# Gating and summing the 16 states of a scan: one wide multiply and one strided reduction in place of 31 narrow operations

## The reference, cut to what matters

```
L, D_MODEL, D_INNER, D_STATE = 2048, 1024, 2048, 16
xz = x @ in_proj_w.T ; x_ssm, z = split(xz)
xc = silu(causal_conv(x_ssm, width 4))
dt_r, Bv, Cv = split(xc @ x_proj_w.T)          # 1, 16 and 16 columns
dt = softplus(dt_r @ dt_proj_w.T + dt_proj_b)
h_t[d, n] = exp(dt_t[d] * A[d, n]) * h_{t-1}[d, n] + dt_t[d] * B_t[n] * xc_t[d]
y_t[d]    = sum over the 16 n of  h_t[d, n] * C_t[n]
y = (y + xc * D) * silu(z) ; out = y @ out_proj_w.T
...
src = layer_norm(src + attention(src))
src = layer_norm(src + relu(src @ W1 + b1) @ W2 + b2)
```

## Time and profile before

| what | us |
|---|---|
| median of 11 runs | 7879.23 (7842.57 to 7989.63) |
| the profiled execution's own time | 7878.18 |
| its span on its slowest core (core 1) | 7876.3 |
| spans of its 8 cores | 7788.7 to 7876.3 |
| VectorE busy | 3911.0 |
| TensorE busy | 2939.3 |
| ScalarE busy | 1959.3 |
| scans L715, first to last start | 368.7 to 3578.6 |

### The profile page before, as it was taken

The page is one execution under the profiler, slowest core; times in us unless marked ns, Lnnn a source line. Parts: engine busy times, 40 slices in busy tenths (PEclk is TensorE's granted clock), DMA queues, the critical chain, the costliest instruction groups (busy, mean ns, idle before and its releaser), DMA issues.

```text
span 7876.3 us, 45497 instructions; the slowest of 8 cores (7788.7 to 7876.3 us)
## 1 busy us (share of the span) xinstructions
PE 2939.3 (37%) x11136; PEld 1122.2 (14%) x11136; DVE 3911.0 (50%) x5725; ACT 1959.3 (25%) x2902; POOL 339.2 (4%) x639
## 2 busy tenths in 40 slices
PE   6300020001100020003506777777757637558272
PEld 3100000000000010001202222222212212223131
DVE  6299947996599839993302221222213343321414
ACT  4223313222233223232213333333330000011112
POOL 0100010001000010000000000000000000000000
PEclk9655565556655575556757777777767768767686
DMA  3400051002300060003781111111111111121211
GB/s 67 52 0 0 0 77 15 0 0 33 59 0 0 3 90 0 0 0 82 83 104 25 20 18 22 17 21 22 21 27 43 55 49 49 42 67 43 75 64 50
DMA packets 100622, 275.49 MB, mean 35 GB/s; under 512 B 19144, under 2 KB 23500, under 8 KB 99084
## 3 DMA queue, kind: packets, MB, share of 16 engines
q0 software_dynamic: 57168, 178.17, 14.6%
q1 hardware_dynamic: 33980, 77.64, 3.2%
q10 hardware_dynamic: 9216, 16.78, 0.6%
HBM read 321.74 MB, written 63.25 MB: 49 GB/s over the span
## 4 chain that ended last, share of the span: by engine, by line
DVE 35%; PE 31%; issue 11%; DMA 10%; ACT 8%; another core or an unknown queue 2%; SPq 1%; DVEq 1%; ACTq 0%; POOL 0%; POOLq 0%
DVE h_band L715 16%; PE psF L1300 6%; PE psF L1519 6%; PE psF L1327 5%; ACT attT L1339 4%; DVE h_band L727 4%; PE psF L1719 3%; PE psF L1731 3%; DMA xreD<-xin 2%; PE psF L1314 2%; DMA wzD<-winp_z 2%; DVE h_band L736 2%; DVE xc_a L1571 2%; PE psF L908 1%
## 5 line engine op out<-in xcount | busy, mean ns | idle before, releaser
L715 DVE TENSOR_TENSOR_SCAN h_band<-daD,hcol,dxD 128x512 f16<-128x512 f32 x1024 | 1302.9, 1278 | 2.3
L626 ACT ACTIVATE daD<-dtD,c_A 128x512 f32<-128x512 f32 x1024 | 732.4, 721 | 1827.7 <-DVE h_band L715 1817.6
L593 PE MATMUL psA<-woD,xc_a 128*128 128x512 bf16 x256 | 69.9, 397 | 2762.4 <-DVE xc_a L765 2726.9
L1339 ACT ACTIVATE attT<-psF 128x1024 bf16<-128x1024 f32 x512 | 498.3, 1022 | 630.8 <-PE psF L1314 624.6
L1388 DVE TENSOR_TENSOR ost<-psF,rlbG 64x512 bf16<-64x512 f32 x64 | 42.4, 680 | 1130.2 <-DMA rlbG<-lrow 547.2
L1300 PE MATMUL psF<-wvG,act_a 128*128 128x512 bf16 x2048 | 491.5, 395 | 175.7 <-DVE ost L1388 147.1
L1519 PE MATMUL psF<-xc_a 128*128 128x512 bf16 x2048 | 475.2, 397 | 30.7 <-DVE xc_a L1571 30.7
L1314 PE MATMUL psF<-qT_aug,kT_aug 65*128 65x512 bf16 x1024 | 381.6, 478 | 208.1 <-ACT attT L1339 204.9
L710 DVE TENSOR_TENSOR dxD<-uD,bb_sb 128x512 bf16<-128x512 bf16 x960 | 407.7, 425 | 95.6 <-DVE h_band L715 2.8
L593 PEld LDWEIGHTS psA<-woD,xc_a 128*128 128x128 bf16 x256 | 22.4, 100 | 2806.8 <-issue 2790.3
L1327 PE MATMUL psF<-attT,v_aug 128*65 128x512 bf16 x1024 | 379.1, 551 | 88.2 <-ACT attT L1339 88.2
(11 more groups left out here) (218 smaller groups left out, 3604.1 us busy)
## 6 DMA issues: line engine op xcount, KB each, us to landing
xc_a<-wob POOLq DMA_DIRECT2D x128, 256.0 KB, 4.7
wzD<-winp_z POOLq DMA_DIRECT2D x64, 256.0 KB, 3.8
woD<-woutT POOLq DMA_DIRECT2D x64, 256.0 KB, 4.7
wob<-wo POOLq DMA_DIRECT2D x1, 16384.0 KB, 298.5
wvG<-wv POOLq DMA_DIRECT2D x32, 512.0 KB, 6.0
xc_a<-w1b POOLq DMA_DIRECT2D x64, 256.0 KB, 6.6
xc_a<-w2b ACTq DMA_DIRECT2D x64, 256.0 KB, 7.9
xreD<-xin SPq DMA_DIRECT2D x16, 512.0 KB, 6.0
```

The lines of the kernel that those rows point to most:

```text
L626: inc(s.activation(daD[n % 2][:], dt[:], AF.Exp, scale=c_A[:, dc * NN + n: dc * NN + n + 1]), "da")
L715: last = v.tensor_tensor_scan(h_band[:, n * TW:(n + 1) * TW], daD[n % 2][:], dxD[n % 2][:], hcol[:, dc * NN + n: dc * NN + n + 1], op0=OP. ...
L1339: inc(s.activation(attT[:, (2 * grp) * 512:(2 * grp + 2) * 512], psF1[:, slot:slot + 1024], AF.Exp, scale=0.125), "gs")
```

## The change

On VectorE, the 16 multiplies become one over the whole 128 x 8192 tile. The 15 additions become one `tensor_reduce` with fp32 output: it reads `h_band` through a pattern whose inner index walks the 16 states of one time step, 512 elements (1024 bytes) apart, and whose outer index walks the 512 time steps. All products are still rounded to fp16; the sum is no longer rounded between additions.

On TensorE, the wait for `ov` 256 ahead of the feed-forward block and the waits for `e3s` inside its loops (4 and 8 in the first half, 12 and 16 in the second) become one wait for `e3s` 16 ahead of it.

```diff
@@ VectorE, for each (tc, dc) @@
-                fg = [0] * NN
-                for n in range(NN):
-                    fg[n] = inc(v.tensor_tensor(h_band[:, n * TW:(n + 1) * TW],
-                                                h_band[:, n * TW:(n + 1) * TW],
-                                                cb_sb[:, n * TW:(n + 1) * TW],
-                                                op=OP.mult), "vf")
-                fl1 = [0] * 8
-                for i8 in range(8):
-                    wge(v, "vf", fg[2 * i8 + 1])
-                    if i8 >= 1:
-                        wge(v, "vf", fl1[i8 // 2])
-                    fl1[i8] = inc(v.tensor_tensor(
-                        h_band[:, i8 * TW:(i8 + 1) * TW],
-                        h_band[:, 2 * i8 * TW:(2 * i8 + 1) * TW],
-                        h_band[:, (2 * i8 + 1) * TW:(2 * i8 + 2) * TW], op=OP.add), "vf")
...
-                wge(v, "vf", fl2[3])
-                f31 = inc(v.tensor_tensor(y_sl[:], h_band[:, 2 * TW:3 * TW],
-                                          h_band[:, 3 * TW:4 * TW], op=OP.add), "vf")
-                wge(v, "vf", f31)
-                fy = inc(v.tensor_tensor(y_sl[:], y_sl[:], h_band[:, 0:TW],
-                                         op=OP.add), "vf")
+                fg = inc(v.tensor_tensor(h_band[:], h_band[:], cb_sb[:],
+                                         op=OP.mult), "vf")
+                wge(v, "vf", fg)
+                fy = inc(v.tensor_reduce(
+                    y_sl[:],
+                    bass.AP(h_band[:].tensor, h_band[:].offset,
+                            [h_band[:].ap[0], [1, TW], [TW, NN]]),
+                    axis=AX.X, op=OP.add), "vf")
                 wge(v, "szs", tc * DC + dc + 1)
                 wge(v, "vf", fy)
@@ TensorE, feed-forward block @@
-        wge(t, "ov", 256)
+        wge(t, "e3s", 16)
         for sh in range(2):
             for r in range(4):
                 ri = sh * 4 + r
                 wge(t, "hw0", 16 * 8 * (ri + 1))
                 wge(t, "hw1", 16 * 8 * (ri + 1))
                 for sc in range(2):
-                    wge(t, "e3s", sh * 8 + (sc + 1) * 4)
                     for m in range(8):
```

More of the change, by code:

```diff
@@ L740, in _ @@
[L740 to L749, removed]
@@ L750, in _ @@
-                f30 = inc(v.tensor_tensor(h_band[:, 0:TW], h_band[:, 0:TW],
-                                          h_band[:, TW:2 * TW], op=OP.add), "vf")
-                wge(v, "vf", fl2[3])
-                f31 = inc(v.tensor_tensor(y_sl[:], h_band[:, 2 * TW:3 * TW],
-                                          h_band[:, 3 * TW:4 * TW], op=OP.add), "vf")
-                wge(v, "vf", f31)
-                fy = inc(v.tensor_tensor(y_sl[:], y_sl[:], h_band[:, 0:TW],
-                                         op=OP.add), "vf")
+                fg = inc(v.tensor_tensor(h_band[:], h_band[:], cb_sb[:],
+                                         op=OP.mult), "vf")
```

## The result

The changed kernel is slower: ratio of the times 1.0537, 95% interval 1.0502 to 1.0571 (medians 8318.58 us of 12 runs against 7901.66 us of 47 runs of the kernel before, both taken over all executions; the ratio leaves out the clearly slower ones, in which TensorE's granted clock was lower, so it isn't the quotient of the medians). The forecast was 8356 us.

The account below looks back on a forecast made before the run. No engine bounds the whole kernel; VectorE paces the scan stage. Per pair 4.56 (multiply) + 15.00 (reduction) - 12.09 (removed) = +7.47 us, times 64 = +478, on 7878 gives 8356 us, range 7945 to 8510.

Parts of the forecast that it names:

- What bounds the scan stage: Scan stage: VectorE sets the pace, ScalarE has slack; L626 waited 1817.6 us on VectorE, L715 idled 2.3 us.
- the stretch: VectorE at each pair's end, first product to L760: 12.09 us, 64 times on the path, to grow to 19.6.
- The multiply: VectorE, one multiply over 8192 columns: 4.46 us, 4.56 with its wait, against 5.38 before; 0.82 us gained.
- The reduction: VectorE, 8192 elements read with 1024-byte jumps at 1.8 ns each: 14.90 us, 15.00 with its wait.
- readings of the carry L721: Carry copy, 16 elements in 176 ns, taken three ways: 2.0, 1.9 or 1.1 ns per element under the jump.
- The free jump: Rival on VectorE's reduction: jumps cost nothing, 8.69 us, +81 us in all, 7959 us; chance 0.28.
- Two elements per step: Rival on VectorE's reduction: two 16-bit elements per step, 4.46 us, -190 us in all, 7688 us; chance 0.03.
- Nothing was hidden: Rival in the scan stage: ScalarE sets the pace, VectorE's longer tail fills waiting time, 7878 us; chance 0.02.
- The jump of more than 2.1 ns: Rival on VectorE's reduction: from 2.1 ns per element it takes 17.35 us, the kernel 8513; chance 0.07.
- The waits: Two per pair on VectorE, both counted; TensorE's feed-forward entrance wait costs nothing, covered by `w2b` loads by 20 us.
- The sum: Scan stage, per pair 4.56 + 15.00 - 12.09 = +7.47 us, times 64 = +478 us, giving 8356 us.

Follow-up runs that it names:

- the run over neighbours: Changed kernel with its reduction reading 16 neighbouring elements per output instead of 16 lying 1024 bytes apart (other sums than the reference's): ratio 1.0094.
- the second timing: Only TensorE's waits at the feed-forward block changed, against the kernel before, timed again after a first 1.0039: ratio 1.0000, interval 0.9976 to 1.0023.

## Why the prediction was right

The time was forecast as 8356 us, and the mechanism was the right one, but the value of its deciding term came near the measured one by luck, as shown under the reduction.

**What bounds the scan stage.** Right. L715's idle time stayed at 2.4 us, L626's wait on VectorE grew from 1817.6 to 2199.0, and the last L593 of core 1 moved from 3632.9 to 4036.8 us, +404 where the stretch says +408. No block hid more than a few us of it.

**The multiply.** Forecast 4.46 us, measured 4.42. It goes at (4425 - 1224) / 6144 = 0.52 ns per column, half the 1.04 of a reduction, and the gain of 0.8 us per pair that was set against the reduction is real: by itself it makes the kernel faster.

**The reduction.** This was the term that decided, and the term that was off: 14.90 us forecast, 13.83 measured, a price of (13834 - 150) / 8192 = 1.67 ns per element where 1.8 was taken. That is 1.07 us per pair, 68 us in all. The mechanism, a price at every jump, held: 0.63 ns on top of 1.04. The way to the number didn't. The 1.8 was chosen from readings of the carry L721 that took 15 to 30 of its 176 ns for reads slowed by the jump, and a copy of 16 neighbours takes 174 to 175 ns as well. Most of what the readings gave to the jump was therefore start. A copy of 16 elements can't tell 1.8 from 1.04, and that the value came within 8% was luck. The prediction also calls the rows that it compared like with like (one source, fp32 out); the longest of them, L1170, writes bf16, and all of them read fp32 where L721 reads fp16. The figure of 1.73 that the prediction quotes from the Trainium skill was the closer one. Row L721 doesn't agree with it in two readings out of three, as was said; it says nothing on it. The chance of 0.60 is given for a price from 1.5 ns, while its own range begins at 1.6; nothing here hangs on that.

**The rivals.** The free jump, with 0.28 the strongest rival, was excluded by the mean of L728, and shown for what it would have been by the run over neighbours, 1.0094 against 7959 / 7878 = 1.0103. Two elements per step is excluded too: a reduction of neighbours takes 1.04 ns for 16-bit input at this length as well. Nothing was hidden. The jump of more than 2.1 ns didn't occur for any pattern tried; the dearest, 14.78 us, is 1.79 ns.

**The waits.** Right, at nothing as far as it can be measured: covered in the trace by 16 us, and 1.0000 in the second timing.

**The sum.** +478 forecast, +408 by the timeline, and a ratio of 1.0537 on 7878 is +423, with 395 to 450 as its interval. The forecast was a loss of 6.1% where 5.4% was measured, too large because of the one term.

## What to carry to other kernels

Fewer and larger instructions win only while each still reads neighbours: here one multiply for 16 gained 0.85 us, and one reduction for 15 additions lost 7.2. Before a tree is folded into a reduction, look at the bytes between two reads of its innermost index: for fp16, with 8 it was free here, from 16 on every read cost 1.67 to 1.79 ns instead of 1.04. Don't take a price per element from a 16-element instruction: with the jump and without, it took 175 and 174 ns. Time a probe of the length that is asked about. And where halves can be added, a tree of wide additions (5.3 us here with its waits) beats even the reduction whose reads are neighbours (8.8 us).

## What the runs showed of the hardware

- The price of a jump is a step and not a slope: 8.69 us for 8192 elements at 2, 4 and 8 bytes, 14.49 and 14.78 at 16 and 32, 13.81 to 13.84 from 64 to 1024.
- Two regions read in turn are free (8.69 us), four are not (13.91).
- A copy that takes two elements per step keeps doing so when it jumps, and pays the extra 0.74 ns once per step (0.43 to 0.62 us for 512 elements), about half as much per element as a reduction (0.63 ns) or a multiply (0.74). At 16 elements it paid 0 to 1 ns. Two jumping sources of one multiply pay it once (1.08 us against 1.07).
- A timing against 26 runs of the kernel before gave 1.0039 with an interval that excluded 1, for an edit that a second timing put at 1.0000. What was seen to vary with no change behind it is TensorE's granted clock in the last stage: 0.72 against 0.82 on two cores of one execution, and 787 against 705 us with it, under the old waits as under the new. That this made the first ratio wasn't shown.
